# Attention stage of a graph kernel: both attention-value products of a pair behind the next pair's logits, with a PSUM bank and result buffers for each graph

## The reference, cut to what matters

```python
normed = _layernorm(hidden, g1, b1)
q, k, v = (normed @ W + b for W, b in ((Wq, bq), (Wk, bk), (Wv, bv)))   # 8 heads of 32
logits = jnp.einsum('bhnd,bhmd->bhnm', q, k) / math.sqrt(Hd)
logits = logits + (2.0 * adj - 1.0)
weights = jax.nn.softmax(logits, axis=-1)
weights = weights * (0.25 + 0.75 * adj)
weights = weights / jnp.maximum(weights.sum(axis=-1, keepdims=True), 1e-06)
attended = jnp.einsum('bhnm,bhmd->bhnd', weights, v)
hidden = hidden + attended.reshape(B, N, D) @ Wo + bo
```

## Time and profile before

| | us |
|---|---|
| median of three runs | 1103.84 |
| lowest and highest run | 1103.62, 1106.32 |
| span of the profiled execution, first to last instruction | 1100.2 |
| median less that span | 3.6 |
| stage A in the profile, first logits to last residual | 27.9 to 412.0 |
| one step of stage A (two halves) in its even part | 23.65 |

### The profile page before, as it was taken

How to read it: one execution, slowest core, us unless ns; L and a number is a source line. 1 busy time by engine, 2 the same in 40 slices (tenths; PEclk the granted TensorE clock), 3 DMA queues, 4 the chain that set the end, 5 groups by cost and what they waited for, 6 DMA issues and landing times.

```text
span 1100.2 us, 39179 instructions
## 1 busy us (share of the span) xinstructions
PE 1042.0 (95%) x15924; PEld 912.7 (83%) x15924; DVE 803.3 (73%) x1935; ACT 714.7 (65%) x1718; POOL 398.2 (36%) x628
## 2 busy tenths in 40 slices
PE   6999999999999989999999999999899999879997
PEld 5888888888888868899989998998778888768886
DVE  4677777777777768865566556655788899859986
ACT  2777667777767755564455445546688888847774
POOL 3531121121121103331123112212478788776552
PEclk9999999999999999999999999999999999989999
DMA  9211111221110002110011011010000000002212
GB/s 246 51 42 41 41 41 41 65 55 41 41 41 12 12 2 59 30 29 20 24 30 25 20 25 30 24 39 10 22 22 19 19 29 20 4 2 78 78 62 93
DMA packets 82476, 43.67 MB, mean 40 GB/s; under 512 B 42912, under 2 KB 77984, under 8 KB 82336
## 3 DMA queue, kind: packets, MB, share of 16 engines
q1 hardware_dynamic: 78016, 41.44, 13.9%
q10 hardware_dynamic: 4320, 0.28, 0.3%
HBM read 21.25 MB, written 12.58 MB: 31 GB/s over the span
## 4 chain that ended last, share of the span: by engine, by line
PE 79%; DVE 8%; issue 5%; POOL 3%; ACT 2%; SPq 1%; DMA 1%; DVEq 0%; POOLq 0%; ACTq 0%
PE BK L1332 8%; PE BK L1334 8%; PE BK L1333 8%; PE BK L1461 6%; PE BK L1435 5%; PE BK L1548 5%; PE BK L1549 5%; PE BK L1550 5%; PE BK L1447 4%; PE BK L1428 3%; PE BK L1348 3%; PE BK L1357 3%; PE BK L1595 3%; PE BK L1349 2%; PE BK L1350 2%
## 5 line engine op out<-in xcount | busy, mean ns | idle before, releaser
L1180 ACT ACTIVATE gf<-BK,bcol 128x512 f32<-128x512 f32 x128 | 88.3, 690 | 159.0 <-PE BK L1334 145.9
L953 POOL TENSOR_TENSOR ve<-mv,eps_l 128x4 f32<-128x4 f32 x64 | 18.3, 285 | 450.4 <-DVE mv L314 418.1
L1096 ACT ACTIVATE e_sb<-BK,nmx 128x128 f32<-128x128 f32 x512 | 142.5, 409 | 28.3 <-DVE nmx L501 28.3
L597 DVE TENSOR_TENSOR gl<-gf,gh 128x512 fp32r<-128x512 f32 x128 | 101.2, 793 | 67.6 <-ACT gh L1181 65.4
L1548 PE MATMUL BK<-wf_hi,gh 128*128 128x256 f32 x512 | 142.5, 278 | 1.8 <-DVE gl L597 1.8
L1549 PE MATMUL BK<-wf_hi,gl 128*128 128x256 f32 x512 | 141.5, 276 | 0.0
L1550 PE MATMUL BK<-wf_lo,gh 128*128 128x256 f32 x512 | 141.5, 276 | 0.0
L507 DVE TENSOR_TENSOR pt_sb<-BK,ft 128x512 f32<-128x512 f32 x128 | 85.2, 686 | 59.8 <-PE BK L1435 58.1
L1116 ACT ACTIVATE xn<-x_all,neg_mr,rstd 128x256 f32<-128x256 f32 (+1 forms) x188 | 103.9, 611 | 4.8 <-POOL neg_mr L962 4.4
L1332 PE MATMUL BK<-xh,wf_hi 128*128 128x512 f32 x256 | 99.8, 390 | 1.3 <-DVE xl L341 0.8
L1334 PE MATMUL BK<-xh,wf_lo 128*128 128x512 f32 x256 | 100.8, 394 | 0.0
(11 more groups left out here) (206 smaller groups left out, 2762.9 us busy)
## 6 DMA issues: line engine op xcount, KB each, us to landing
x_all<-in_x_dram SPq DMA_DIRECT2D x16, 512.0 KB, 4.7
out_dram<-y SPq DMA_DIRECT2D x16, 512.0 KB, 2.9
xn<-tb_ln SPq DMA_DIRECT2D x240, 32.0 KB, 1.9
adj_in<-in_adj_dram SPq DMA_DIRECT2D x64, 64.0 KB, 3.5
adj_kept<-adj_tr SPq DMA_DIRECT2D x16, 256.0 KB, 2.4
adj_in<-adj_kept SPq DMA_DIRECT2D x16, 256.0 KB, 2.6
s_wf<-in_L_gnn_Wf_dram SPq DMA_DIRECT2D x2, 1024.0 KB, 6.8
s_w<-in_L_gnn_W_dram SPq DMA_DIRECT2D x2, 256.0 KB, 2.9
```

The costliest lines, as they stand in the source:

```text
L597: dve.tensor_tensor(gl[:, f, :], gf[f % 2][:], gh[:, f, :].bitcast(F32), ALU.subtract).then_inc(b_gl, 1)
L1096: e = act.activation(e_sb[:, j, :], LE[:, r, q, :], ACT.Exp, bias=nmx[:, j:j + 1], scale=1.0)
```

## The change

Three things are changed. First, each graph of a pair gets its own PSUM bank (4 or 5) for its attention-value product, its turned result and its projected result, and its own `att` and `att_t`. Second, the later work on a pair is no longer spread over a half one graph after the other: both `a_av` stand directly behind the logits, both `a_attn_turn` behind the first `a_turn`, and both `a_out` follow; DVE's `a_norm` and ACT's `a_att_copy` come in pairs accordingly. Third, other work is moved around them: on ACT `ln_hi` goes behind the first exponentials and `a_adj` behind the second `a_qk_out`; on DVE the statistics of chunk i+1 are split over the two halves, `aggr` goes from the end of half 0 into half 1 behind `a_resid(s)`, and `a_ft_out`, `adj_turn` move to half 1. No instruction is added or taken away in a step. The residual of the last graph of a pair now falls into the same half.

```diff
-        O_ps = BK[:, 4, 0:H * HA].rearrange("p (h c) -> p h c", c=HA)
+        O_ps = [BK[:, 4 + r, 0:H * HA].rearrange("p (h c) -> p h c", c=HA) for r in range(2)]
-        AT_ps = BK[:, 4, 0:D]
-        WO_ps = BK[:, 5, 0:D]
+        AT_ps = [BK[:, 4 + r, 0:D] for r in range(2)]
+        WO_ps = [BK[:, 4 + r, D:2 * D] for r in range(2)]
...
 DVE, a_step
                     if not first:
                         a_max(sp, 0)
+                    if back:
+                        a_norm(s)
+                        a_norm(s + 1)
                     if pp == 0 and not first:
                         ln_lo(i + CA)
                     if not first:
                         a_max(sp, 1)
+                        a_pt_out(sp, 1 - par, pp, 0)
                     if back:
-                        a_norm(s - 2)
-                    if old:
-                        a_resid(*((i - 2, 1) if pp == 0 else (i - 2, 3)), s - 3)
-                    if not first:
-                        a_pt_out(sp, 1 - par, pp, 0)
-                    if pp == 0 and not tail:
-                        a_ft_out(i, par)
+                        a_resid(s)
+                    if pp == 1 and not tail:
+                        a_stats(i, half, par, (2, 3))
+                        dve.wait_ge(ln_st, (i + CA + 2) * G)
+                        aggr(i + CA + 1)
                     if not first:
                         a_pt_out(sp, 1 - par, pp, 1)
-                    if pp == 1 and not (isinstance(i, int) and i >= NC - 1):
-                        adj_turn(half + par, 1 - par)
-                    if pp == 0 and not tail:
-                        a_stats(i, half, par, (0, 1))
-                        if isinstance(i, int) and i == 1:
-                            setup_biases()
                     if back:
-                        a_norm(s - 1)
+                        a_resid(s + 1)
+                    if pp == 1 and not tail:
+                        a_ft_out(i, par)
                     if not first:
                         a_pt_out(sp, 1 - par, pp, 2)
                         a_pt_out(sp, 1 - par, pp, 3)
                     if pp == 0 and not tail:
-                        a_stats(i, half, par, (2, 3))
-                        dve.wait_ge(ln_st, (i + CA + 2) * G)
-                    if back:
-                        a_resid(*((i - 2, 2) if pp == 0 else (i - 1, 0)), s - 2)
-                    if pp == 0 and not tail:
-                        aggr(i + CA + 1)
+                        a_stats(i, half, par, (0, 1))
+                    if pp == 0 and i == 1:
+                        setup_biases()
+                    if pp == 1 and i < NC - 1:
+                        adj_turn(half + par, 1 - par)
...
 ACT, a_step
-                    if pp == 0:
+                    if first and pp == 0:
                         ln_hi(i + CA)
                     if not first:
                         a_exps(sp, 0)
+                    if not first and pp == 0:
+                        ln_hi(i + CA)
                     if pp == 0 and not tail:
-                        a_adj(i, par)
                         if first:
+                            a_adj(i, par)
                             act.wait_ge(setup_dve, setup_at["projections"])
                     if not first:
                         a_exps(sp, 1)
-                    if pp == 1 and not tail:
-                        a_qk_out(i, par, 3)
                     if back:
-                        a_att_copy(s - 2)
-                    if pp == 0 and not tail:
-                        a_qk_out(i, par, 0)
-                    if pp == 1 and not tail:
-                        normalise(i, CA, (0, 1))
+                        a_att_copy(s)
+                        a_att_copy(s + 1)
+                    if not tail:
+                        if pp == 0:
+                            a_qk_out(i, par, 0)
+                        else:
+                            a_qk_out(i, par, 3)
+                            normalise(i, CA, (0, 1))
                     if not first:
                         a_exps(sp, 2)
                         a_exps(sp, 3)
...
 PE, a_step
                     if not first:
                         a_logits(sp, i - 1, 1 - par, pp)
+                    if back:
+                        a_av(s, sp - 1)
+                        a_av(s + 1, sp - 1)
                     if pp == 0:
                         wait_for(pe, a_vev, i * 2)
                         ln_turn(i + CA)
...
-                    if back:
-                        a_av(s - 2, sp - 1, *before, 0)
-                    if old:
-                        a_out(s - 3)
...
+                    if pp == 1 and not tail:
+                        a_proj(i, 3)
                     if not first:
                         a_turn(sp, 0)
+                    if back:
+                        a_attn_turn(s)
+                        a_attn_turn(s + 1)
...
+                    if pp == 1 and not tail:
+                        a_vproj(i, 0)
+                        a_vproj(i, 1)
+                    if back:
+                        a_out(s)
+                        a_out(s + 1)
                     if pp == 0 and not tail:
                         a_proj(i, 0)
-                    if back:
-                        a_attn_turn(s - 2)
-                    if pp == 1 and not tail:
-                        a_vproj(i, 0)
                     if not first:
                         a_turn(sp, 1)
-                    if back:
-                        a_av(s - 1, sp - 1, *before, 1)
-                        a_out(s - 2)
                     if not tail:
                         if pp == 0:
                             a_proj(i, 1)
                         else:
-                            a_vproj(i, 1)
                             a_vproj(i, 2)
                     if not first:
                         a_turn(sp, 2)
                         a_turn(sp, 3)
-                    if back:
-                        a_attn_turn(s - 1)
                     if not tail:
                         if pp == 0:
                             a_proj(i, 2)
```

More of the change, by code:

```diff
@@ L109, in build @@
         xl = sb("xl", [P, KT, W4], F32R)
-        REGION = 60 * 1024
+        REGION = 61 * 1024 + 512
         base_of_region = (nc.sbuf_base + 31) // 32 * 32
@@ L133, in build @@
         bv_col = o("bv_col", [P, KT])
+        bv_wide = o("bv_wide", [P, KT, P])
         o = overlay(base_of_x + 6 * G * D * 4, base_of_x + 10 * G * D * 4)
@@ L144, in build @@
         pt_sb = [o(f"pt_sb{r}", [P, 2 * H, P]) for r in range(2)]
-        att = o("att", [P, D])
-        att_t = o("att_t", [P, D])
+        att = [o(f"att{r}", [P, D]) for r in range(2)]
+        att_t = [o(f"att_t{r}", [P, D]) for r in range(2)]
         nmx = o("nmx", [P, 2 * H])
@@ L149, in build @@
         rinv = o("rinv", [P, H])
-        bv_wide = o("bv_wide", [P, KT, P])
         o = overlay(base_of_region, base_of_region + REGION)
@@ L510, in a_norm @@
             def a_norm(s):
+                r = s % 2
                 dve.wait_ge(a_o, s + 1)
-                dve.tensor_scalar(rsum[:], O_ps[:, :, HD], 1e-6, None, ALU.max).then_inc(a_rs, 1)
+                dve.tensor_scalar(rsum[:], O_ps[r][:, :, HD], 1e-6, None, ALU.max).then_inc(a_rs, 1)
                 dve.wait_ge(a_rs, s + 1)
@@ L515, in a_norm, with a_resid @@
                 dve.wait_ge(a_ri, s + 1)
-                wait_for(dve, a_at, s)
-                dve.tensor_tensor(att[:].rearrange("p (h d) -> p h d", d=HD), O_ps[:, :, 0:HD],
+                wait_for(dve, a_at, s - 1)
+                dve.tensor_tensor(att[r][:].rearrange("p (h d) -> p h d", d=HD), O_ps[r][:, :, 0:HD],
                                   rinv[:].unsqueeze(2).to_broadcast([P, H, HD]), ALU.mult).then_inc(a_att, 1)
-            def a_resid(i, g, s):
+            def a_resid(s):
                 dve.wait_ge(a_wo, s + 1)
-                dve.wait_ge(a_xb, i * G + g + 1)
-                dve.tensor_tensor(xs(i, g), WO_ps, xs(i, g), ALU.add).then_inc(a_x, 1)
+                dve.wait_ge(a_xb, s + 1)
+                dve.tensor_tensor(xs(s // G, s % G), WO_ps[s % 2], xs(s // G, s % G), ALU.add).then_inc(a_x, 1)
             def a_stats(i, half, par, graphs):
@@ L538, in a_step @@
             def a_step(i, half, par):
-                first, tail = (isinstance(i, int) and i == n for n in (0, NC))
+                first, tail = i == 0, i == NC
                 for pp in range(2):
-                    s, sp = i * G + (2 * pp - G), i * 2 + (pp - 2)
-                    back = not (isinstance(s, int) and s < 2)
-                    old = not (isinstance(s, int) and s < 3)
+                    sp = i * 2 + (pp - 2)
+                    s = 2 * sp - 2
+                    back = sp >= 1
                     if not first:
                         a_max(sp, 0)
+                    if back:
+                        a_norm(s)
+                        a_norm(s + 1)
                     if pp == 0 and not first:
@@ L581, in _ @@
```

(68 more changed lines are left out.)

## The result

The changed kernel takes 1225.99 us (median of four runs, 1220.99 to 1228.35) beside 1103.73 for the kernel before; the ratio is 1.108, 95% interval 1.106 to 1.111. The forecast was 1206 (1172 to 1231). The profiled execution has a span of 1222.1, 121.9 more than before, and nearly all of that lies in stage A: its first gelu in stage B comes at 535.67 us in place of 413.83.

What follows compares the result with a forecast made beforehand. TensorE was taken to bound stage A, so only order mattered. Half 1 67.5, half 0 23.8, end -1.3 and clock 12 sum to 102 us on 1103.8, giving 1206, range 1172 to 1231.

Steps and rivals of the forecast that it cites:

- Half 1: Stage A, half 1: late statistics hold `normalise` and exponential quarters 2 and 3 behind it; 4.5 us in steps 1-15, 67.5 us.
- Half 0: Stage A, half 0: late copies delay `a_out`, `a_proj(0)`, the q copy and quarters 2, 3; 1.7 us a step, 23.8 us.
- Clock: Half 1: PE's 4.1 us idle drops its clock to half rate each step; 0.8 us in 15 steps, 12 us.
- My own prices: PE in half 1 at half clock: quarter 3 ends 0.3 later, last `a_vproj` ends at 16.6, past 15.7.
- the upper bound: Clock fall reaching the next logits, 1.8 us a step, 27 us; with 10 for longer handovers, added to 1194: 1231.
- the sum: Whole kernel: 67.5 + 23.8 - 1.3 + 12 = 102 us added to 1103.8, giving 1206.
- End: Last half of stage A: the final pair's work overlaps across the banks, 14.7 us in place of 16.07, -1.3.
- Rival (c): PE's queue: faster through five fewer shape changes a step and covered waits; 10 us gain, 1094; chance 0.03.
- Hidden parts: Moved `a_adj`, `adj_turn`, adjacency loads, first two statistics and POOL's bias additions cost nothing; second bank only takes waits away.

Runs made afterwards that it cites:

- Both ways of undoing the wait: Changed kernel with all four statistics and `aggr` back at half 0's end: 1154.15 us; or with exponential quarters 2 and 3 ahead of `normalise` in half 1: 1153.58.
- gap filled: Changed kernel, same order, plus 15 extra matmuls with unused results in PE's long wait of half 1, each step: 1213.31 us, ratio 1.095.
- early statistics: Changed kernel with DVE taking all four statistics of chunk i+1 and `aggr` at the end of half 0 again: 1154.15 us, ratio 1.042.

## Why the prediction was right, step by step

- **Half 1: right in mechanism and size.** Forecast 15.7 without the clock, measured 15.50; the idle times forecast for ACT (5.0) and PE (4.1) were 4.75 and 3.73. In step 15 POOL began 8.91 us into the half (forecast 9.10), quarter 2 of the exponentials 11.80 (12.0). Both ways of undoing the wait take 72 us off, but this holds the clock's fall as well. By the clean halves the wait itself is 15.50 less 11.48, 4.0 us a half; the other 0.3 over 11.18 are not the wait's.
- **Half 0: right.** Forecast 14.2, measured 14.17 when clean (gap filled); the wait for the copies was forecast as 1.6 and is 1.2. The copies' part, 0.93 of the 1.7, is shown by the run that moves them; that the rest goes by `a_proj(0)`, the q copy and quarter 2 fits the 3.4 us a step that ACT waits for q, but was not tried alone.
- **Clock: the fall was right, its place half wrong.** I took 0.8 in half 1 and nothing for the next logits, which I put only into the upper bound. My own prices give 0.9 a step (16.6 less 15.7), not 0.8. In fact the low stretch reaches past half 1 in most steps. With the gap filled, halves 0 of steps 2 to 15 shrink by 9.2 us in total and halves 1 by 8.4, although the stops in them grew by 2.6 and 1.2. So the fall costs some 21 us there (an estimate from these sums), and full clock brings some of it back as stops. That the 12 us of the sum lie next to the 12.7 of the median is luck. The Trainium skill ("TensorE: Matmul & The Clock Gate", section "HAM oscillation") has the rule that idle time between bursts costs the clock anew in each pass. The trace agrees: the granted clock is 0.85 to 0.96 in each half 1 of steps 1 to 15.
- **End: right.** Forecast 14.7, measured 14.99.
- **Missing from the sum: the stops in PE's own instructions.** In steps 1 to 15 PE is idle for 10.4 us in ten stops of over 0.4 us: the 5.5 and 3.5 of the list of waits, and one of 1.4 in step 1. They and the half-clock logits make up most of the 20 us between 1206 and 1226. The upper bound held such logits and 10 us for handovers, but no stops: that 1226 still lies under 1231 is in part luck.
- **Rival (c)** fell as argued: `normalise` does wait. Whether fewer changes of shape save PE time is not shown. With early statistics PE is busy for 10.75 in half 1 against 11.07 before, but for 12.41 in half 0 against 12.32 before, and that half 1 took 11.48, longer than 11.18. The Trainium skill ("TensorEngine Tiling (Array Packing)", section "Key Properties") says that a change of tiling mode drains TensorE. Half 1 agrees in sign, half 0 does not.
- **Hidden parts**: that the second bank only takes waits away fits the run with the banks alone, 0.5% faster. `adj_turn`, `a_adj` and the adjacency loads show no wait in the list of waits.
- **A misreading without effect**: I gave DVE and ACT 1.2 to 3 us of slack in each half. By the earlier trace rows it is 2.5 to 3.5; the 1.2 is PEld's. The sum does not use it.

## What to carry to other kernels

Before moving an instruction that waits, write down what stands behind it on the same engine: here a normalisation that was not needed for another half held exponentials that were needed at once. The same kind of wait was cheap behind the work that did not need it and dear ahead of it, and moving it (one line) was worth as much as making its data early. PE had hardly any gaps before, and the new orders won at most half a microsecond in a half; of what was tried, the relaxed buffers alone gave a gain.

## What the runs showed of the hardware that was not expected

PE stops in the middle of its own work, and the traces point to the loading of its program. In the changed kernel's half 1 of step 11 the logits start at 364.47, both products follow, and PE stops six instructions before their end:

```profile
364.47 1.17 PE L1426 MATMUL BK<-k,q 32*128 32x128 f32 x32
365.57 1.32 PE L1447 MATMUL BK<-v,pt_sb 128*32 128x33 f32 x122
368.31 0.26 PE L1447 MATMUL BK<-v,pt_sb 128*32 128x33 f32 x6 [1.42 <-issue]
```

In the six microseconds from 364 the DMA view has two instruction transfers, of 16 KB each:

```profile
q8 instruction: 2, 0.03, 2.2%
```

One of them runs from 365.76 to 366.78, and PE goes on 1.53 us after its end. The same holds for all ten stops of over 0.4 us in steps 1 to 15: a 16 KB transfer begins 1.0 to 2.4 us ahead of the idle time, and PE goes on 1.1 to 1.5 us after the transfer has ended. The stops also lie at even distances in the program. Counting PE's matmuls, weight loads and semaphore instructions in the trace, from the end of one stop to the end of the next there are 256 times 10, 2, 5, 10, 2, 5, 5, 5 and 2 instructions, to within two. Two of these stretches, with the numbers of matmuls and weight loads in brackets:

```profile
417.33:463.01 45.68, 37.42 (x634) 31.11 (x635) 27.78 (x60) 25.78 (x77) 4.41 (x8) 0.96 0.09 24
463.01:480.93 17.92, 13.48 (x254) 11.87 (x254) 10.08 (x26) 9.36 (x30) 4.42 (x8) 0.90 0.05 17
```

In the kernel before, where at most one product follows the logits, the waits by issue at the products are short in steps 3 to 15:

```profile
PEld BK L1447 <- issue: 8.7, 39, 0.3
```

Logits and two products are 64 + 256 instructions, weight loads counted, in about 2.4 us. With `a_proj(3)` between logits and products, or between the products, no stop of over 0.4 us is left in steps 2 to 15; with `ln_turn` (about 1 us) between, some are. That PE waits there for the next 256 instructions of its program, and that the 16 KB transfer brings them, is an inference from the distances, from the transfers and from what removes the stops. It would also say why only some bursts stop: in the others no such block ends late in the burst, or the burst is slower (half-clock logits in steps 3 and 8). The rate at which the program can be loaded was not measured.
